# The second layer's product with the weight, from scaled 16-bit parts in place of f32

## What is computed

```python
# layer 0
norm2 = jnp.linalg.norm(x, axis=1, keepdims=True)
cos = beta[0] * (x @ x.T) / (norm2 @ norm2.T + 1e-07)
P = jax.nn.softmax(cos + (1.0 - adj) * -1000000000.0, axis=1)
x = _layernorm(x + P @ x, axis=-1)
# layer 1
output = jnp.matmul(adj, jnp.matmul(x, weight))
x = _layernorm(x + output, axis=-1)
```

## Time and profile before

| | us |
|---|---|
| median of 3 runs | 491.95 (489.52 to 493.45) |
| profiled execution | 490.71 |
| its span | 488.9 |
| TensorE busy (weight loads) | 466.7 (304.5) |
| VectorE, ScalarE, GpSimd busy | 371.4, 319.4, 58.3 |
| layer 1 (364.6 to 488.9) | 124.3 |

### The profile page before, as it was taken

One profiled execution on the slowest core, in us unless ns is written; L12 is line 12 of the kernel. 1 busy time (PEld: TensorE's weight loads), 2 busy tenths in 40 slices (PEclk: granted clock), 3 DMA queues, 4 the chain that ended last, 5 costly groups with the idle time before them and its releaser, 6 DMA issues.

```text
span 488.9 us, 8865 instructions
## 1 busy us (share of the span) xinstructions
PE 466.7 (95%) x3495; PEld 304.5 (62%) x3495; DVE 371.4 (76%) x583; ACT 319.4 (65%) x374; POOL 58.3 (12%) x75
## 2 busy tenths in 40 slices
PE   1889989999999999999999999999989999999995
PEld 1456757667666767676676676676764455545484
DVE  4889969999999999999999999999963022210252
ACT  5889968898898889889888988987961000000000
POOL 5711010210110020110102002000100000000011
PEclk9989999999999999999999999999999999999999
DMA  8999979999999999999996997950052010011111
GB/s 197 105 115 112 135 100 127 121 147 156 119 158 129 138 152 113 154 144 80 170 127 90 159 112 124 94 142 22 0 174 86 1 43 23 21 44 44 44 42 46
DMA packets 103386, 50.20 MB, mean 103 GB/s; under 512 B 69536, under 2 KB 99904, under 8 KB 103360
## 3 DMA queue, kind: packets, MB, share of 16 engines
q0 software_dynamic: 19536, 16.78, 41.0%
q1 hardware_dynamic: 83536, 33.06, 33.0%
q10 hardware_dynamic: 288, 0.07, 0.1%
HBM read 77.40 MB, written 22.82 MB: 205 GB/s over the span
## 4 chain that ended last, share of the span: by engine, by line
PE 81%; DMA 12%; POOL 2%; DVE 2%; issue 2%; ACT 1%; POOLq 0%; SPq 0%; DVEq 0%; ACTq 0%
PE psum L1020 22%; PE psum L955 19%; PE psum L959 10%; PE psum L932 9%; PE psum L930 9%; PE psum L931 9%; DMA adjT<-adj_bytes 5%; DMA adj_bytes<-in_adj 5%; POOL rn L395 1%; PE psum L1036 1%; DMA adjT<-in_x 1%; DVE E L708 1%; DVE el L716 1%; ACT eh L487 1%; ACT E L478 1%
## 5 line engine op out<-in xcount | busy, mean ns | idle before, releaser
L955 PE MATMUL psum<-xaug,eh 128*128 128x257 f16 x1024 | 184.5, 274 | 3.0 <-DVE el L716 3.0
L478 ACT ACTIVATE E<-psum,sc 128x1024 f32<-128x1024 f32 x128 | 154.2, 1205 | 39.0 <-PE psum L932 38.0
L959 PE MATMUL psum<-xaug,el 128*128 128x129 f16 x1024 | 175.6, 221 | 0.0
L708 DVE SCALAR_TENSOR_TENSOR E<-E,adjT 128x1024 f32<-128x1024 f32 x128 | 156.0, 1219 | 13.3 <-ACT E L478 8.2
L716 DVE SCALAR_TENSOR_TENSOR el<-E,eh 128x1024 f16<-128x1024 f32 x128 | 155.6, 1216 | 0.0
L487 ACT ACTIVATE eh<-E 128x1024 f16<-128x1024 f32 x128 | 134.4, 1050 | 4.4 <-DVE E L708 3.8
L955 PEld LDWEIGHTS psum<-xaug,eh 128*128 128x128 f16 x1024 | 99.4, 98 | 28.0 <-DVE el L716 3.7
L1020 PE MATMUL psum<-adjT,uT 128*128 128x512 fp8e4 (+1 forms) x576 | 112.1, 355 | 0.0
L959 PEld LDWEIGHTS psum<-xaug,el 128*128 128x128 f16 x1024 | 100.3, 98 | 14.4
L930 PE MATMUL psum<-uT 128*128 (+1 forms) x256 | 98.9, 386 | 0.2 <-DVE uT L599 0.2
L931 PE MATMUL psum<-uT 128*128 (+1 forms) x256 | 98.7, 386 | 0.0
(11 more groups left out here) (75 smaller groups left out, 160.4 us busy)
## 6 DMA issues: line engine op xcount, KB each, us to landing
adj_bytes<-in_adj POOLq DMA_DIRECT2D x28, 512.0 KB, 12.6
xres<-in_x SPq DMA_DIRECT2D x8, 256.0 KB, 3.2
q_row<-norms SPq DMA_DIRECT2D x8, 256.0 KB, 8.2
x_rows<-x SPq DMA_DIRECT2D x8, 256.0 KB, 3.2
E<-x_rows SPq DMA_DIRECT2D x8, 256.0 KB, 3.0
out<-E SPq DMA_DIRECT2D x16, 128.0 KB, 2.2
adj_bytes<-in_adj POOLq DMA_DIRECT2D x7, 256.0 KB, 6.4
x_parts<-x1p SPq DMA_DIRECT2D x7, 256.0 KB, 4.0
```

What stands on the lines that cost most here:

```text
L478: nc.scalar.activation(E[:, m % RING, :, :], S[m % 2], ACT.Exp, bias=col(C_BB), scale=col(C_BS)).then_inc(e_done, 1)
L708: nc.vector.scalar_tensor_tensor(out=e, in0=e, scalar=EPRE, in1=mask_bytes(b, m), op0=ALU.mult, op1=ALU.min).then_inc(masked, 1)
L955: return nc.tensor.matmul(O[t][:, 0:XC], eh[:, s, a, cols], xaug[:, j, :], start=start, stop=stop)
L959: return nc.tensor.matmul(O[t][:, 0:D + 1], el[:, s, a, cols], xaug[:, j, 0:D + 1], start=False, stop=False)
```

## The change

The product of blocks 0 to 6 is made from f16 parts. Both factors get a high and a low part. The sums are scaled by 2^-11: ACT writes the high part (in the place of the f32 copy), then DVE the low part (`sum_low`, new), into the first two slots of `eh`. The weight is scaled by a power of two worked out on the chip from its largest absolute value, which takes a reduction at the start, a third column in the two small transposes, and five small DVE operations after layer 0; its parts lie side by side in `el`, 256 columns. For each tile there are then two matmuls: the sums' high part with both parts of the weight, and the sums' low part with the weight's high part. `C` becomes two banks for each slot, and DVE adds both column halves with their scale to the residual, in two instructions instead of one. The last block (both halves) keeps f32. ACT's wait for `c_done` before the last block goes, since `sumT` has no other use then. TensorE's wait for `o_read` moves ahead of the loop, as `C[1]` is now banks 6 and 7.

```diff
...
+        sum_parts_of = eh[:, 0:2, :, :]
+        w_parts = el[:, 0, 0, 0:2 * D]
+
         def mask_bytes(b, m):
             return adjT[:, b, m, :].bitcast(U8).rearrange("p (i a) -> p a i", a=2)
 
         def adj_cols(r, j, cols):
             return adjT[:, r, j // 2, :].bitcast(F8).rearrange("p (i a) -> p a i", a=2)[:, j % 2, cols]
 
-        C_G0, C_G1, C_PX, C_XS, C_XI, C_B, C_BS, C_BB, C_T2 = range(9)
+        C_G0, C_G1, C_GW, C_PX, C_XS, C_XI, C_B, C_BS, C_BB, C_T2, C_WI, C_WS, C_WU = range(13)
 
         def col(c):
             return sc[:, c:c + 1]
...
         S = [psum[:, 2 * s:2 * s + 2, :] for s in range(2)]
         O = [psum[:, 4 + t, :] for t in range(IT)]
         BT = [psum[:, s, :] for s in range(2)]
-        C = [psum[:, 2 + s, :] for s in range(2)]
+
+        C = [psum[:, 2 + 4 * s:4 + 4 * s, :].rearrange("p b (k c) -> p (b k) c", c=2 * D) for s in range(2)]
         BT_half = [BT[1], O[0]]
-        C_half = C[1]
-        C_last = [O[1], O[2]]
+        C_half = psum[:, 6, :]
+        C_last = [O[1], O[3]]
...
             act.wait_ge(s_filled, NPAIR)
             split_x1_hi(NB - 1)
 
+            act.wait_ge(w_scale, 5)
+            nc.scalar.activation(w_parts[:, 0:D], w_sb[:, :], ACT.Copy, scale=col(C_WS)).then_inc(w_hi, 1)
             for r in range(NB - 1):
                 act.wait_ge(agg_done, r + 1)
                 if r > 1:
                     act.wait_ge(c_done, r - 1)
-                nc.scalar.activation(sumT[:, r % 2, :], BT[r % 2], ACT.Copy).then_inc(sum_moved, 1)
-            act.wait_ge(c_done, NB - 2)
+                nc.scalar.activation(sum_parts_of[:, r % 2, 0, :], BT[r % 2], ACT.Copy, scale=SSC).then_inc(sum_hi, 1)
             for half in range(2):
                 act.wait_ge(half_summed, half + 1)
                 nc.scalar.activation(sumT[:, 1, half * HB:(half + 1) * HB], BT_half[half][:, 0:HB],
-                                     ACT.Copy).then_inc(sum_moved, 1)
+                                     ACT.Copy).then_inc(half_moved, 1)
 
         @block.vector
         def _(dve):
...
 
             def partition_extremes():
 
+
+                dve.wait_ge(w_in, 16)
+                dve.wait_ge(consts, 5)
+                nc.vector.tensor_reduce(ext[:, 2:3], w_sb[:, :], AX.X, ALU.max, apply_absolute_value=True).then_inc(ext_step, 1)
                 dve.wait_ge(n2_done, NC)
-                dve.wait_ge(consts, 5)
                 nc.vector.tensor_scalar_mul(neg[:, :], n2[:, :], -1.0).then_inc(ext_step, 1)
                 nc.vector.reduce_max(ext[:, 0:1], n2[:, :], AX.X).then_inc(ext_step, 1)
-                dve.wait_ge(ext_step, 1)
+                dve.wait_ge(ext_step, 2)
                 nc.vector.reduce_max(ext[:, 1:2], neg[:, :], AX.X).then_inc(ext_step, 1)
 
             def extremes():
                 dve.wait_ge(ext_turned, 1)
                 nc.vector.reduce_max(ext_all[:, :], ext_turn, AX.X).then_inc(ext_step, 1)
-                dve.wait_ge(ext_step, 4)
+                dve.wait_ge(ext_step, 5)
                 nc.vector.tensor_copy(ext_rows[:, :], ext_all[:, :].to_broadcast([NT, P])).then_inc(ext_spread, 1)
 
             px = col(C_PX).bitcast(I32)
 
             def tiny_norms():
                 dve.wait_ge(rows_turned, 1)
-                nc.vector.tensor_copy(sc[:, C_G0:C_G1 + 1], rows_turn[:, 0:2]).then_inc(maxima, 1)
+                nc.vector.tensor_copy(sc[:, C_G0:C_GW + 1], rows_turn[:, 0:3]).then_inc(maxima, 1)
                 dve.wait_ge(maxima, 1)
                 nc.vector.tensor_scalar(flag[:, :], col(C_G1), -2.0, None, ALU.is_gt).then_inc(flag_set, 1)
                 nc.vector.tensor_scalar(px, col(C_G0).bitcast(I32), 0x7F800000, 1, ALU.bitwise_and,
...
             row_shift(b)
             split_x1_lo(b)
 
+
+            wi = col(C_WI)
+            nc.vector.tensor_scalar_max(wi, col(C_GW), 2.0 ** -100).then_inc(w_scale, 1)
+            dve.wait_ge(w_scale, 1)
+            nc.vector.tensor_scalar(wi.bitcast(I32), wi.bitcast(I32), 0x7F800000, None, ALU.bitwise_and).then_inc(w_scale, 1)
+            dve.wait_ge(w_scale, 2)
+            nc.vector.tensor_scalar_mul(wi, wi, 2.0 ** -13).then_inc(w_scale, 1)
+            dve.wait_ge(w_scale, 3)
+            nc.vector.tensor_scalar_mul(col(C_WU), wi, 1.0 / SSC).then_inc(w_scale, 1)
+            nc.vector.reciprocal(col(C_WS), wi).then_inc(w_scale, 1)
+            dve.wait_ge(w_hi, 1)
+            nc.vector.scalar_tensor_tensor(out=w_parts[:, D:2 * D], in0=w_sb[:, :], scalar=col(C_WS),
+                                           in1=w_parts[:, 0:D], op0=ALU.mult, op1=ALU.subtract).then_inc(w_lo, 1)
+
+            def sum_low(r):
+                dve.wait_ge(sum_hi, r + 1)
+                nc.vector.scalar_tensor_tensor(out=sum_parts_of[:, r % 2, 1, :], in0=BT[r % 2], scalar=SSC,
+                                               in1=sum_parts_of[:, r % 2, 0, :], op0=ALU.mult,
+                                               op1=ALU.subtract).then_inc(sum_moved, 1)
+
             def normalise_rows(slot, ts, src):
                 for t in ts:
                     o = IT * slot + t
...
                                                    rstd[:, o:o + 1], ALU.subtract, ALU.mult)
                 last.then_inc(y_done, 1)
 
+            sum_low(0)
+            sum_low(1)
             for r in range(NB - 1):
                 slot = r % 2
                 base = 5 * NB + 2 * r
                 st = stage[:, slot, :, :]
                 dve.wait_ge(c_done, r + 1)
                 dve.wait_ge(x1_in[slot], 16 * (r // 2 + 1))
-                nc.vector.tensor_tensor(st[:, :, D:2 * D], C[slot].rearrange("p (t d) -> p t d", d=D),
-                                        st[:, :, 0:D], ALU.add).then_inc(c_read, 1)
+                nc.vector.scalar_tensor_tensor(out=st[:, :, D:2 * D], in0=C[slot][:, :, 0:D], scalar=col(C_WU),
+                                               in1=st[:, :, 0:D], op0=ALU.mult, op1=ALU.add).then_inc(c_added, 1)
+                dve.wait_ge(c_added, r + 1)
+                nc.vector.scalar_tensor_tensor(out=st[:, :, D:2 * D], in0=C[slot][:, :, D:2 * D], scalar=col(C_WU),
+                                               in1=st[:, :, D:2 * D], op0=ALU.mult, op1=ALU.add).then_inc(c_read, 1)
                 dve.wait_ge(c_read, r + 1)
                 moments(lambda t: st[:, t, D:2 * D], IT * slot, range(IT), base)
                 dve.wait_ge(chain, base + 1)
...
                 if r > 1:
                     dve.wait_ge(y_stored[slot], 32 * (r // 2))
                 normalise_rows(slot, range(IT), lambda t: st[:, t, D:2 * D])
+                if r + 2 < NB - 1:
+                    sum_low(r + 2)
 
 
             st = stage[:, 1, :, :]
...
 
             turn_unit_rows(0)
             turn_unit_rows(1)
-            pe.wait_ge(ext_step, 3)
+            pe.wait_ge(ext_step, 4)
             nc.tensor.transpose(ext_turn, ext[:, :], ident[:, :]).then_inc(ext_turned, 1)
 
             def turn_extremes():
...
                 for t in ts:
                     nc.tensor.matmul(C_last[t - HT][:, 0:D], ident[:, :], stage[:, 1, t, 0:D], start=True, stop=False)
 
-            def weights(r, out, ts, n):
-                pe.wait_ge(sum_moved, n)
+            def weights(r):
+                pe.wait_ge(sum_moved, r + 1)
                 if r > 1:
                     pe.wait_ge(c_read, r - 1)
-                for k, t in enumerate(ts):
+                for t in range(IT):
                     cols = slice(t // 2 * HB + t % 2, (t // 2 + 1) * HB, 2)
-                    last = nc.tensor.matmul(out[:, k * P:(k + 1) * P], sumT[:, r % 2, cols], w_sb[:, :],
-                                            start=True, stop=True)
+                    nc.tensor.matmul(C[r % 2][:, t, :], sum_parts_of[:, r % 2, 0, cols], w_parts, start=True, stop=False)
+                    last = nc.tensor.matmul(C[r % 2][:, t, 0:D], sum_parts_of[:, r % 2, 1, cols], w_parts[:, 0:D],
+                                            start=False, stop=True)
                 last.then_inc(c_done, 1)
 
 
...
             pe.wait_ge(x1_split, NB)
             aggregate(0, range(NT - IT, NT), BT[0]).then_inc(agg_done, 1)
             aggregate(1, range(NT - IT, NT), BT[1]).then_inc(agg_done, 1)
+            pe.wait_ge(w_lo, 1)
+
+            pe.wait_ge(o_read, 2 * NB)
             for r in range(2, NB - 1):
 
-                weights(r - 2, C[r % 2], range(IT), r - 1)
+                weights(r - 2)
                 aggregate(r, range(0, NT), BT[r % 2]).then_inc(agg_done, 1)
             r = NB - 1
-            weights(r - 2, C[r % 2], range(IT), r - 1)
+            weights(r - 2)
             aggregate(r, range(0, NT // 4), BT_half[0][:, 0:HB], slice(0, HB))
-            weights(r - 1, C[(r - 1) % 2], range(IT), r)
+            weights(r - 1)
             aggregate(r, range(NT // 4, NT), BT_half[0][:, 0:HB], slice(0, HB)).then_inc(half_summed, 1)
-            pe.wait_ge(o_read, 2 * NB)
```

(20 more changed lines are left out.)

## The result

The changed kernel takes 488.27 us (median of 20 runs, 487.02 to 490.46); the kernel before, now with 20 runs, 489.57 us (488.48 to 493.45). The ratio is 0.9959, with a 95% interval of 0.9941 to 0.9978: 0.4% faster, small but clear of the scatter. In two further comparisons the same pair gave 0.9977 (0.9960 to 0.9993) and 0.9986 (0.9950 to 1.0023). Over all runs on record of the two kernels, 73 before and 38 changed, the medians are 489.5 and 488.2 us, so the change is worth about 1.3 us (0.6 to 1.7 when the runs are resampled). The profiled execution took 489.05 us with a span of 487.1; the span before was 488.9.

A forecast was written before the change was run, and what follows sets the result against it. TensorE was taken as the bound, with the product directly on its path. Terms -1.8 + 0 + 0 + 0 + 0 us took the profiled execution to 488.9 us and the median from 491.95 to 490.2 us, range 488.0 to 492.1.

The forecast's parts named there:

- Part 1: Product blocks on TensorE: seven blocks fall from 0.93 to 0.67 us, saving 1.8 us, bounds 0.9 to 2.0.
- Part 2: Split of the sums on ACT and DVE: low part takes 0.69 us, cost 0, at most 0.2 at the first block.
- Part 3: DVE between blocks: each chain ends about 1.4 us later against TensorE, hidden until the end, cost 0.
- the cover: Time at the end between DVE finishing the half block and the last product being ready: 1.6 us left.
- Part 4: The weight's own split, seven small DVE and ACT operations after layer 0: done before 380 us, cost 0.
- Part 5: One more weight reduction on DVE at the start, 0.25 us: cost 0, or 0.25 us with its cover gone.
- The chances: Odds on the whole kernel's measured time against the kernel before: faster 0.06, same 0.90, slower 0.04.
- the 1% bound: For the whole kernel's time: about 1% (4.9 us) is what can be told from no change.

The follow-up runs named there:

- Experiments 2: Changed kernel with the product put back to one f32 matmul a tile, splits and both adds kept: 490.31 us against 489.64 for the kernel before, ratio 1.0017.
- experiment 3: Kernel before, with each f32 product of blocks 0 to 6 made twice: 496.37 us against 489.64, ratio 1.0135.
- Experiment 7: Changed kernel with two or four more DVE operations over 128x512 after each block's adds: 487.72 us (two) and 490.81 us (four), against 489.72 for the kernel before.
- experiment 4: Changed kernel with three f16 matmuls of 128 columns a tile and one DVE add a block: 488.22 us against 489.64 for the kernel before, ratio 0.9971.
- experiment 8: Changed kernel with block 1's second mask cast issued later: 488.42 us beside 488.14; also with three-matmul product and weight reduction moved: 488.40 us.
- experiment 6: Changed kernel without the weight's reduction at the start (constant scale), run twice: 486.16 us, then 487.65 us beside 488.14 for the changed kernel.

## Why the prediction was right in its steps and wrong in its number

**Part 1, right; sized 0.1 us low.** Forecast 0.67 us a block and 1.8 us in all; measured 0.66 and 1.9 (0.27 x 7). Experiments 2 and 3 show that the blocks are the whole gain from the first product on and lie bare on the path. The pairs L955/L959 were the right row to price from; their record lengths (0.274 and 0.221 us) would have made a block three times as long, 2.0 us. The Trainium skill's four passes for a true FP32 product ("FP8 and Floating Point Precision", TensorE Precision Notes) gave an estimate of 1.5 us; the measured f32 tile takes 0.2325 us, and each one added in experiment 3 takes 0.2375, against 0.213 for the passes, so the row and not the rule had the size.

**Part 2, right.** The timeline of the changed kernel at the first block, beside the earlier trace rows:

```profile
390.84 0.60 ACT L573 ACTIVATE eh<-psum 128x512 f16<-128x512 f32 x1 [14.89 <-PE psum L1062]
391.47 0.69 DVE L881 SCALAR_TENSOR_TENSOR eh<-psum,eh 128x512 f16<-128x512 f32 x1 [15.13 <-ACT eh L573]
392.27 0.10 PEld L1078 LDWEIGHTS psum<-el,eh 128*128 128x128 f16 x1 [0.24 <-issue]
```

The low part ends at 392.16, the weight load follows at 392.27, and the product's turn in the chain is 392.53: no cost. At the seventh block there is no wait either. The low part took 0.692 us, forecast 0.69.

**Part 3, right, with the mechanism where it was put.** T, the end of the sixth block, is 464.91 (the aggregation's end in the chain) + 0.66 = 465.57. The x1 load was issued at T + 8.7 and had landed at T + 11.7, half 0 was done at T + 14.6 and the last product at T + 16.3; forecast were 8.7, 11.7, 14.7 and 16.35. The wait that the change brings in, 0.65 us for the x1 rows, is the one forecast and costs nothing. Experiment 7 measured the cover at 1.9 us; I had 1.6.

**Part 4, right.** The weight's split ended at 376.34, sixteen microseconds ahead of its use at 392.27.

**Part 5, neither shown nor refuted.** The reduction took 0.29 us, and the first scores came 0.19 us later, but no earlier without it (13.65 and 13.73 us against 13.68). Its removal gained 2 us in three runs, with no lower clock in the trace, and 0.5 in six. The medians put the first product 0.6 us later with the change, more than the 0.25 us that I gave as the most; whether the start or chance did that is open.

**The number failed in one step above all: "the median is 1.24 us more; the saving is carried over to it unchanged."** The sum against the profiled execution was right (span 487.1 forecast, 487.1 measured), but the median of three runs was no firm ground: with twenty it is 489.57, not 491.95. 490.2 us therefore names a time above the kernel before as it really is, and the range from 488.0 to 492.1 reaches above the highest of the changed kernel's twenty runs (490.46), while at the low end it holds the median by 0.3 us only. I had the warning in hand, a profiled execution 1.24 us under the median, and gave that difference away. Had I carried 1.9 us to 489.6, I would have said 487.7, which is still 0.6 us under the measured 488.27: "carried over unchanged" failed too, since the medians gained 1.3 us and the stretch 1.9. The span of 487.1 came out to the tenth only because the two profiled executions happened to agree ahead of the first product.

**The chances were right by the 1% bound** (0.4% is within it) and still told too little: I took 1% for what a measurement of this kernel can tell. Twenty runs told 0.4% from nothing, with an interval of 0.2% on each side. The sum already said 0.4%, with bounds of one sign, and still only 0.06 went to "faster"; the text should have said "faster, by less than 1%".

## What to carry to other kernels

Price a matmul by the distance between starts in a run of the same form, not by the length of its record, and look in the chain of waits whether the block lies bare; then a gain of 0.4% in that stretch can be forecast to a tenth of a microsecond. Before adding it to a median, find the part of the trace that scatters and the event after which it no longer does, ask how many runs the median has, and look at the granted clock there as well as at the waits. When an engine off the path gets more work, look for the last two of its chains that run back to back: there the delays add, and the cover at the end has to hold both.

## What the runs showed that I had not expected

In experiment 4 a weight load of 128x128 f16 needs no more than 0.056 us beside matmuls of 128 columns: twelve loads and twelve matmuls in 0.67 us, with loads recorded as 0.10 us each. The Trainium skill ("TensorE: Matmul & The Clock Gate", Wait — 56ns, not 53.3ns?) gives 55.6 ns from start to start at 128 columns for back-to-back matmuls, and this trace agrees, with a load for every matmul (0.67 / 12 = 0.056).

A 128 KB store took 3.45 us to land in experiment 4 and 4.05 in the kernel with both edits of experiment 8, where the same one takes 2.2 in the changed kernel, and the 256 KB load behind it took 4.24 us in the second run of experiment 6 and not 3.0. Half 0 waits for that load, and the end still came within 0.1 us of its place (stretches of 94.7, 94.7 and 94.6 us): the cover took it up.
